# Turning back and selecting at a greater distance in the first two passes of a four-layer graph network

## The reference

```
layer 0, twice: msg = x[src] @ W_msg + edge_attr_32 @ W_edge
                x1  = leaky_relu(seg_max(msg, dst) + x @ W_root + b)
layer 1:        w   = relu(edge_attr_17 @ W1.T + b1) @ W2.T + b2
                out = relu(x @ Ws.T + bs + seg_sum(w * x[src], dst) @ Wn.T + bn)
layer 2:        two hops h = seg_sum(norm * h[src], dst)
layer 3:        seg_sum(scaled x[src], dst) @ W, scaled, + bias
after each layer: x = layernorm(x + layer(x))
```

## Time and profile before

| | |
|---|---|
| median of 3 runs | 4723.26 us (4720.13 to 4724.09) |
| profiled execution | 4718.38 us, span 4716.6 us |
| TensorE busy | 3549.1 us, 75% |
| VectorE busy | 2500.2 us, 53% |
| GpSimd busy | 2376.2 us, 50% |
| ScalarE busy | 929.8 us, 20% |
| gather L930, 2496 | 948 ns each |
| scan L2293 | 1271 ns each |
| selection's hot rows L2298, 416 | 558 ns each |
| window one-hots L2324 and L2326 | 411 and 273 ns each |
| window products L1245, 1600 | 373 ns each |

### The profile page before, as it was taken

The page is one execution under the profiler, slowest core; times in us unless marked ns, Lnnn a source line. Parts: engine busy times, 40 slices in busy tenths (PEclk is TensorE's granted clock), DMA queues, the critical chain, the costliest instruction groups (busy, mean ns, idle before and its releaser), DMA issues.

```text
span 4716.6 us, 64730 instructions
## 1 busy us (share of the span) xinstructions
PE 3549.1 (75%) x23472; PEld 2740.7 (58%) x23472; DVE 2500.2 (53%) x6368; ACT 929.8 (20%) x2714; POOL 2376.2 (50%) x2520
## 2 busy tenths in 40 slices
PE   3666776677647777777776676777777789999999
PEld 2444554454424544454444454555555569999999
DVE  4555666565636666666665455555555553232211
ACT  0100000000112222222222232332232230011100
POOL 5566666666466666666664566665565640000000
PEclk6788777777868888888887788878888889999999
DMA  5323232323223333333332222233333338777776
GB/s 148 100 63 73 63 73 65 72 62 73 60 66 104 97 102 98 101 102 106 97 103 67 68 78 70 76 90 93 105 105 103 103 98 267 275 255 257 257 275 241
DMA packets 192519, 555.56 MB, mean 118 GB/s; under 512 B 77782, under 2 KB 83382, under 8 KB 172662
## 3 DMA queue, kind: packets, MB, share of 16 engines
q1 hardware_dynamic: 67132, 335.46, 22.3%
q0 software_dynamic: 80432, 124.45, 12.8%
q10 hardware_dynamic: 44682, 92.08, 5.2%
HBM read 455.53 MB, written 96.37 MB: 117 GB/s over the span
## 4 chain that ended last, share of the span: by engine, by line
PE 46%; another core or an unknown queue 23%; DVE 14%; issue 9%; ACT 5%; ACTq 2%; DMA 1%; DVEq 0%; SPq 0%
PE banks L1443 17%; PE banks L1217 7%; PE banks L1173 5%; DVE scan L2293 5%; PE banks L1245 4%; DVE hot_key L2324 3%; PE banks L1170 3%; PE banks L1357 3%; PE banks L1189 3%; DVE hot_src L2326 2%; PE banks L1365 2%; ACT adj L1710 1%; DVE back L2298 1%; DVE hot_lo L1952 1%
## 5 line engine op out<-in xcount | busy, mean ns | idle before, releaser
L930 POOL DMA_INDIRECT gath<-table,ids x2496 | 2365.8, 948 | 1476.3 <-issue 687.2
L1217 PE MATMUL banks<-back 128*96 128x104 f32 (+11 forms) x6000 | 783.5, 279 | 180.3 <-issue 128.4
L1217 PEld LDWEIGHTS banks<-back 128*96 128x96 f32 x6000 | 721.5, 191 | 253.5 <-issue 185.3
L2324 DVE TENSOR_SCALAR hot_key<-banks,key_t 128x392 bf16<-128x392 int16 x1600 | 658.2, 411 | 315.2 <-remote 292.6
L1443 PE MATMUL banks<-r_parts,adj_in 128*128 128x288 bf16 x6543 | 809.6, 286 | 4.6 <-DMA adj_in<-adjacency 4.6
L1245 PE MATMUL banks<-hot_key,hot_src 128*128 128x392 bf16 x1600 | 459.1, 373 | 468.1 <-ACT adj L1710 292.5
L1443 PEld LDWEIGHTS banks<-r_parts,adj_in 128*128 128x128 bf16 x6543 | 802.4, 143 | 6.4 <-issue 4.4
L2293 DVE TENSOR_TENSOR_SCAN scan<-keep_of,scan,banks 96x512 f32<-96x512 bf16 x414 | 526.3, 1271 | 407.7 <-remote 320.5
L1245 PEld LDWEIGHTS banks<-hot_key,hot_src 128*128 128x128 bf16 x1600 | 149.3, 108 | 786.6 <-issue 726.0
L1173 PE MATMUL banks<-ea_of,w_edge_of 128*96 128x512 f32 x832 | 546.9, 742 | 18.3 <-issue 17.4
L1709 ACT ACTIVATE adj<-banks 128x160 bf16<-128x160 f32 x800 | 242.4, 303 | 1109.8 <-remote 720.3
(11 more groups left out here) (182 smaller groups left out, 2382.5 us busy)
## 6 DMA issues: line engine op xcount, KB each, us to landing
adj_in<-adjacency SPq DMA_DIRECT2D x114, 1568.0 KB, 6.5
adjacency<-adj ACTq DMA_DIRECT2D x100, 464.0 KB
gath<-table,ids POOLq DMA_INDIRECT x2496
ea_of<-in_ea_t SPq DMA_DIRECT2D x78, 512.0 KB
keep_of<-keep_max_d SPq DMA_DIRECT2D x52, 768.0 KB
adjacency<-adj ACTq DMA_DIRECT2D x100, 320.0 KB
adj_in<-adjacency SPq DMA_DIRECT2D x33, 928.0 KB, 4.8
ahead_of<-adjacency SPq DMA_DIRECT2D x33, 640.0 KB
```

Of the source, the lines that this page charges most:

```text
L930: pool.indirect_dma_start(gath[:, b, t, :], None, tables[p][:, :], bass.IndirectOffsetOnAxis(ap=ids[:, 1, n:n + 1], axis=0),).then_inc(s_g ...
L1217: m = pe.matmul(band_ps[g % 2][:, at:at + n], rows_in[:, q % 2, t * D:(t + 1) * D], hot_dst[:, q % 2, t, first:first + n], start=False, st ...
L2324: ve.tensor_scalar(hot_key[:, h, a, :], key_places_ps, key_t[:, 0, a, bass.ds(n, 1)], None, ALU.is_equal)
```

## The change

Turning back comes two steps after the turning (`STEP_LAG` 2) and the selection four (`SELECT_LAG`, new). `hot_dst` has three buffers in these passes, chosen by `hots_at`. The waits of `hots_of_ends` and `one_hots` follow the new distances. The histogram's count keeps its distance of one step. The selection stands before the turning back in a step. In pass 1, `window_hots` stands last in VectorE's step, and both windows' products and copies stand last in the steps of TensorE and ScalarE.

```diff
-STEP_LAG = 1
+STEP_LAG = 2
+SELECT_LAG = 4
...
-            hot_dst = of_back[:, 2 * QT * D:2 * QT * (D + WIDE)].rearrange("p (h t c) -> p h t c", h=2, t=QT)
+            hot_dst = of_back[:, 2 * QT * D:QT * (2 * D + 3 * WIDE)].rearrange("p (h t c) -> p h t c", h=3, t=QT)
...
-            ready = s - later - (STEP_LAG + 1 if IS_MAX[p] else 0)
+            ready = s - later - (SELECT_LAG if IS_MAX[p] else 0)
...
+        def hots_at(p, q):
+
+            return q % (3 if IS_MAX[p] else 2)
...
-                            for g in starting(s - STEP_LAG - 3):
+                            for g in starting(s - SELECT_LAG - 2):
...
-                                          hot_dst[:, q % 2, t, first:first + n],
+                                          hot_dst[:, hots_at(p, q), t, first:first + n],
...
TensorE
                         if s < QUARTERS:
                             turn(p, s)
-                        for i, k in windows_at(p, s, 1):
-                            count_window(p, i, k, 0)
-                        if p == 0 and STEP_LAG <= s < QUARTERS + STEP_LAG:
-                            count(s - STEP_LAG)
+                        if p == 0 and 1 <= s <= QUARTERS:
+                            count(s - 1)
+                        if SELECT_LAG <= s < QUARTERS + SELECT_LAG:
+                            select_ends(p, s - SELECT_LAG)
                         if STEP_LAG <= s < QUARTERS + STEP_LAG:
                             turn_back(p, s - STEP_LAG)
-                        if STEP_LAG < s <= QUARTERS + STEP_LAG:
-                            select_ends(p, s - STEP_LAG - 1)
...
                         for i, k in windows_at(p, s, 1):
+                            count_window(p, i, k, 0)
                             count_window(p, i, k, 1)
...
ScalarE
                     for s in range(QUARTERS + TAIL):
-                        for i, k in windows_at(p, s, 1):
-                            take_window(p, i, k, 0)
                         if STEP_LAG <= s < QUARTERS + STEP_LAG:
                             evacuate(p, s - STEP_LAG)
...
                         for i, k in windows_at(p, s, 1):
+                            take_window(p, i, k, 0)
                             take_window(p, i, k, 1)
...
VectorE
-                    if q + 1 < QUARTERS:
-                        ve.wait_ge(s_turn, QUARTERS * p + q + 2)
+                    if q + STEP_LAG < QUARTERS:
+                        ve.wait_ge(s_turn, QUARTERS * p + q + STEP_LAG + 1)
                     else:
-                        ve.wait_ge(s_back, QUARTERS * p + q + 1)
-                    hots_in_span(q, rel_end).then_inc(s_hot_end, 1)
+                        ve.wait_ge(s_back, QUARTERS * p + q)
+                    hots_in_span(p, q, rel_end).then_inc(s_hot_end, 1)
 
                 def one_hots(q):
-                    if q >= 2:
-                        ve.wait_ge(s_back, q - 1)
+                    if q == 2:
+                        ve.wait_ge(s_turn, q + 1)
+                    elif q > 2:
+                        ve.wait_ge(s_back, q - STEP_LAG)
...
                     for s in range(QUARTERS + TAIL):
-                        for i, k in windows_at(p, s, 0):
-                            window_hots(p, i, k)
                         if p == 0 and s < QUARTERS:
                             one_hots(s)
...
+                        for i, k in windows_at(p, s, 0):
+                            window_hots(p, i, k)
```

More of the change, by code:

```diff
@@ L275, in gnn_kernel @@
             msg_now = back_of
-            hot_dst = of_back[:, 2 * QT * D:2 * QT * (D + WIDE)].rearrange("p (h t c) -> p h t c", h=2, t=QT)
-            root_in = of_back[0:D + 1, 2 * QT * (D + WIDE):2 * QT * (D + WIDE) + BAND]
-            band_in = of_back[0:D, 2 * QT * (D + WIDE) + BAND:2 * QT * (D + WIDE) + 2 * BAND]
+            hot_dst = of_back[:, 2 * QT * D:QT * (2 * D + 3 * WIDE)].rearrange("p (h t c) -> p h t c", h=3, t=QT)
+            root_in = of_back[0:D + 1, QT * (2 * D + 3 * WIDE):QT * (2 * D + 3 * WIDE) + BAND]
+            band_in = of_back[0:D, QT * (2 * D + 3 * WIDE) + BAND:QT * (2 * D + 3 * WIDE) + 2 * BAND]
             with ExitStack() as of_general:
@@ L2294, in scan_quarter, with hots_in_span @@
                                           start, ALU.min, ALU.max).then_inc(s_scan, 1)
-                def hots_in_span(q, of):
-                    return ve.tensor_tensor(hot_dst[:, q % 2, :, :],
+                def hots_in_span(p, q, of):
+                    return ve.tensor_tensor(hot_dst[:, hots_at(p, q), :, :],
                                             of[:, QT * q:QT * (q + 1)].unsqueeze(2).to_broadcast([P, QT, WIDE]),
@@ L2473, in message @@
                         ve.wait_ge(s_sel, sums_marked(2, q - 2))
-                    hots_in_span(q, flag)
+                    hots_in_span(2, q, flag)
                     ve.wait_ge(s_w, q + 1)
```

## The result

The kernel before takes 4722.8 us (median of 20 runs, 4717.9 to 4727.5), the changed one 4729.6 (20 runs, 4722.1 to 4737.1): ratio 1.0017, 95% interval 1.0011 to 1.0023. The forecast was 59 us less. The profiled execution of the changed kernel took 4722.1 us, its span is 4720.3. What came is the rival "No change", with the 7 us that the ends of the passes cost.

A forecast was written before the change was run, and what follows sets the result against it. GpSimd's gather floor plus pauses from TensorE's late semaphores was taken to bound the first two passes. -42 - 21 + 4 = -59 us gave 4659 profiled, 4664 us as median; range 4575 to 4745.

The forecast's parts named there:

- No change: Rival, chance 0.14: what holds the semaphores holds TensorE too, so each pause still frees two turnings; 4722 us.
- What bounds the kernel: First two passes: GpSimd's 5.0 us a quarter plus 2.1 us pauses, 212 and 206 us a pass, from late turnings.
- D: Delay of a handoff from TensorE, products' end to scan: 4.8 us in a first-pass example, 4.9 in the second.
- First pass, turning back and selection: Longer distances free a fifth of 100 pauses, 20 of 2.1 us: -42 us, bounds 0 and -212.
- Second pass: Window products last, scan ahead of the one-hots: 10 pauses of 2.1 us fewer, -21 us.
- VectorE in the first pass: One-hots and hot rows wait for older turnings, with a third buffer: 0, between -3.4 and +3.4 us.
- Ends: Ends of two passes: two more quarters of selection after the last turning, +4 us, between 0 and +8.
- the row with 75.6 us of idleness without a releaser: First pass, TensorE's idle time at L1217 with no releaser: 75.6 us, against 49.2 put down to the copy.
- Big gain: Rival, chance 0.17: pauses are a matter of depth alone, half of 418 us goes; 4518 us.
- Slower: Rival, chance 0.24: second-pass loop of 6.2 us + D over two steps decides from D = 5.6 us; 4775 us.
- The clock: Rival without its own chance: TensorE standing less could lift the first pass's 0.78; counts only by pauses saved.

The follow-up runs named there:

- the job run again: Kernel before and changed kernel, both unchanged, measured again in a later job: 4762.7 and 4767.0 us, ratio 1.0007.
- the run of 16 gathers shown: Kernel before with GpSimd waiting for the turnings once in four quarters instead of at each, first two passes: 5219.2 us, ratio 1.1073.
- the paced gathers: Changed kernel, GpSimd also waiting ahead of a quarter's second gather until the quarter before landed: 4521.9 us, ratio 1.12; the kernel before with this wait: 4501.5.

## Why the prediction was wrong

*What bounds the kernel: right.* GpSimd's floor of 1.25 us a gather, pauses on top, D in TensorE's signals. Where D is gone, the passes with all their gathers lie on that floor.

*First pass, turning back and selection, -42 us: this step failed.* It said "One more turning can be in flight when held semaphores come, so that some bursts of two quarters become three". The stall was taken away (49.2 to 0.2 us) and 100 pauses stayed 100, 212.8 to 210.4 us, with 15 runs of three quarters where 16 had been. I had priced a pause by a stall on TensorE, while a pause comes from the run of gathers itself: in its first 8 us TensorE and VectorE get their work done, then TensorE's instructions come one by one and its signals wait until GpSimd stops. Even a quarter of TensorE's work away bought 33 us. That two quarters fit between pauses because two steps of 3.4 us fill those 8 us is my reading of it and was not tested by itself; that three fit with less work for TensorE agrees with it.

*Second pass, -21 us: failed in the same way.* 288.3 us ahead of hot_key became 341.5 ahead of the scan. The order in which VectorE does its work at a pause's end doesn't matter if it waits for the same pause. Pauses went from 97 to 106 (215.1 to 222.9 us).

*VectorE in the first pass, 0:* nothing speaks against it (743.7 and 741.3 us busy; gathers over 1223.1 and 1222.3 us), but no run takes it by itself.

*Ends, +4 us with bounds 0 and 8: right in kind,* 6.8 us, and 4.7 in the job run again. They have the size of the 7 us (and of the 4 us of that job), which is as far as it is shown.

*The rivals.* "No change" gave 4722 and is what happened, for its reason: what holds the semaphores holds TensorE as well. It deserved more than 0.14: the row with 75.6 us of idleness without a releaser said so. "Big gain" is what the Trainium skill's rule on TensorE's ports (SBUF — State Buffer, "SBUF: two separate sides") would give. The measurement decides: where signals are held, neither more distance nor less work brings it. The plain DMAs with more traffic held nothing, as the rule has it, so what holds TensorE beside indirect gathers is something that the rule doesn't tell of. "Slower" needed a D of over 5.6 us in the second pass, and it did not come: from the end of a turning's products to its scan it was 3.5 us before and 3.8 after at the median, 4.0 and 3.5 on average. The prediction's 4.9 us for the second pass also held 1.05 us in which VectorE made one-hots ahead of the scan. The clock fell instead of rising, without weight.

## What to carry to other kernels

Before a stall is priced, ask what makes it end: here most waits of four engines ended together, in the pauses of the engine that issues gathers, and taking one of them away only let another stand there. An idle time without a releaser on an engine that has work queued can be the sign that it is held by something that no reordering reaches; the test is to take the suspected cause away (a quarter of the gathers gave 19%), not to shorten what waits. And a kernel should be measured in more than one job, since its bound can be another one.

## What the runs showed of the hardware

In the jobs at 4717 to 4763 us, beside indirect gathers that GpSimd issues back to back (1.25 us each), TensorE's busy share falls after some 8 us (in one stretch to a matmul in 0.7 to 1.4 us), and its signals arrive late: 1.5 to 2 us at the median, one in ten over 6 us, and 16 us in the run of 16 gathers shown, 2.2 us after the last of them. With plain DMAs of the same bytes from the same queue, or one gather in four, this is gone (0.01 us), for 3824 and 3846 us in place of 4717 and 4762, while it stays in the third pass of the same executions.

The same kernel took 4717 to 4763 us in four jobs, that of the result among them, and 4040 in two, and chip number 9 gave both. In the six traces from the jobs at 4040 us no more than 3 of TensorE's 2282 signals were over 0.1 us late, beside up to 832 gathers without a pause; the kernel before itself has no trace there. What decides whether gathers hold signals stays open, and so does the way in which they do it. The change was never timed by itself where they don't; with a lead of four quarters it made no difference there, and with the paced gathers it took 20 us more.
